# Expert feed-forward kernel: the sums of weights and of gathered rows move from GpSimd to VectorE

## The chip, the cores and the metric

The kernel runs on one core of one Trainium2 chip. The metric is the device time of one execution in microseconds (us), from three timed runs. One more execution was recorded by the hardware profiler; the rows quoted below are from that one.

## The reference, cut to what matters

The program computes a cross-attention layer and then a mixture of 8 experts, each a gated feed-forward network. Every one of the 4096 tokens goes to 2 experts. Only the second part is touched by the change:

```
x_rep_sort = take(x_flat, sort_idx // 2)              # rows gathered by expert
h   = silu(ragged_dot(x_rep_sort, w1)) * ragged_dot(x_rep_sort, w3)   # 1024 -> 3584
out = ragged_dot(h, w2)                                # 3584 -> 1024
out = sum over the token's 2 experts of weight * out
```

## The kernel before, in words

`attend_and_route` does the attention and writes tables of rows by expert (the first 555 us). `experts` then works through slots. A slot is one expert with up to 1088 of its rows. With these inputs 8 slots are filled.

**Products.** Every fp32 operand is split into a high part and a low rest of type fp32r, and each product is made of three matmuls: high by high, high by low, low by high. ScalarE copies the high part (`weight_hi`, `w2_hi`, `h_hi`, `rows_hi`, all at L1042), and VectorE subtracts it from the operand to get the low part (`weight_lo`, `w2_lo`, `h_lo`, `rows_lo`, all recorded at L1238). The tiles are `wh`/`wl` for weights and hidden values and `xh`/`xl` for rows.

**Units.** The first half of a slot (matmul L1462) is 28 units, 14 column pairs of w1 and of w3 in turn (a = 0, 1). A unit is a 2x2 block product done with 7 products in place of 8 (Winograd's form of Strassen's scheme). So it needs four sums of weight blocks (`sums`, four buffers) and, once for a slot, four sums of blocks of gathered rows. VectorE combines the seven products from PSUM (L1241, L1275) and multiplies by the gate (L1261). While TensorE works on one unit, ScalarE and VectorE split the weights of the next: entry e of `wh`/`wl` is refilled once product e is done.

**Down passes.** The second half (matmul L1495) is 4 passes (c = 0 to 3) of 28 steps. A step t needs a tile of w2 (256 KB) and of the stored hidden values (272 KB). Its buffers are one of two: SyncE loads tile t once `w2_lo` and `h_lo` of t-2 are done, ScalarE splits it once TensorE finished step t-2. A step of TensorE has 12 matmuls in the slots with at most 512 columns (slots 0, 1, 3, 5, "narrow" below) and 24 in the others (2, 4, 6, 7, "wide"). After a pass the result is turned back (`turn_back`, L1562), multiplied (`rows_out`, L1332) and added to the output by five indirect DMAs (`scatter`, L1722). Within the passes the rows of the next slot are prepared: gathered by GpSimd's indirect DMAs (`gather`, L1704), turned by TensorE (`turn_rows`, L1543), copied by ScalarE into the four `sums` buffers, split, summed and split again. `rows_hi` and `rows_lo` stand between the steps in an order written out by hand.

**Who forms the sums before.** GpSimd, in `weight_sums` (L1653 to L1661), `row_sums` (L1668 to L1674) and `tail_sums` (L1681 to L1687, the last rows of a slot). GpSimd's queue in a slot is, in order: the weight sums of 13 pairs; records and the first gather; then for each pass c the gather for c+1, `row_sums` of c, in pass 1 `tail_sums`, and, for c > 0, `scatter` of pass c-1; then the first weight sums of the next slot, `scatter` of pass 3, and four more weight sums. `row_sums` waits for `rows_lo` 0 and then 2 of the same pass, and `tail_sums` for `tail_lo` 0 and 2, so each `scatter` stands in the queue behind these. In pass 3 SyncE also loads the next expert's first weights (`load13`, L972, two DMAs of 1 MB each), one behind the loads of step 7 and one behind those of step 15.

Of the kernel before, what the change touches and what calls it, by code (L numbers as in the profile page):

```python
# [21 lines left out]
P = 128  # L22
# [803 lines left out]
def experts(nc, w1, w3, w2, out, x2_rows, table, meta, raw13, s_raw13):  # L826

    with ExitStack() as st:
# [405 lines left out]
        def _(dve):  # L1234
# [7 lines left out]

            def weight_lo(s, i, a, e):
# [8 lines left out]
            def unit(s, i, a, cols, after):  # L1252
# [96 lines left out]
            def down_phase(s, cols):  # L1349
# [7 lines left out]
                for c in range(4):  # L1357
# [3 lines left out]
                    rows_lo(n + c, c, 1, steady)  # L1361
                    steps(t + 4, t + 5)
                    rows_lo(n + c, c, 2, steady)
                    for i in range(3, EP):
                        steps(t + 2 * i, t + 2 * i + 2) if i > 3 else steps(t + 5, t + 8)
                        rows_lo(n + c, c, i, steady)
                    if c == 1:
                        steps(t + 14, t + 15)
                        for i in range(3):
                            tail_lo(s + 1, i)  # L1370
                        steps(t + 15, t + 16)
                        for i in range(3, EP):
                            tail_lo(s + 1, i)
                        steps(t + 16, t + MT)
                    else:
                        steps(t + 14, t + MT)
# [12 lines left out]
            def slot(s, cols):  # L1389

                with dve.Fori(0, PAIRS - 1) as i:
                    unit(s, i, 0, cols, lambda e: weight_lo(s, i, 1, e))
                    unit(s, i, 1, cols, lambda e: weight_lo(s, i + 1, 0, e))
                i = PAIRS - 1
                unit(s, i, 0, cols, lambda e: weight_lo(s, i, 1, e))
# [7 lines left out]
                unit(s, i, 1, cols, begin_down)  # L1403
# [22 lines left out]
            for c in range(4):  # L1426
                for i in range(EP):
                    rows_lo(c, c, i, first_q[c % 2])
            for i in range(EP):
# [202 lines left out]
        def _(pool):  # L1632
# [7 lines left out]
            def weight_sums(s, i, a, fresh=False):  # L1640

                A11, A12, A21, A22 = (raw13[a][:, kh * KH:(kh + 1) * KH, mt * P:(mt + 1) * P]
                                      for mt in range(2) for kh in range(2))
                before = s * PRODUCTS + i * (2 * EP) + a * EP - EP
                done = s * (PAIRS * 8) + i * 8 + a * 4
                pool.wait_ge(s_raw13[a], s * (PAIRS * 16) + i * 16 + 16)

                def free(e):
                    if not fresh:
                        pool.wait_ge(s_wlo, before + e + 1)  # L1650

                free(1)
                G.tensor_tensor(sums[:, 0, :, :], A11, A21, ALU.subtract).then_inc(s_sum, 1)  # L1653
                free(4)
                G.tensor_tensor(sums[:, 1, :, :], A21, A22, ALU.add).then_inc(s_sum, 1)  # L1655
                pool.wait_ge(s_sum, done + 2)
                free(2)
                G.tensor_tensor(sums[:, 2, :, :], sums[:, 1, :, :], A11, ALU.subtract).then_inc(s_sum, 1)  # L1658
                pool.wait_ge(s_sum, done + 3)
                free(5)  # L1660
                G.tensor_tensor(sums[:, 3, :, :], A12, sums[:, 2, :, :], ALU.subtract).then_inc(s_sum, 1)  # L1661

            def row_sums(n, quads):

                x11, x21, x12, x22 = quads
                pool.wait_ge(s_quad, n * 4 + 4)
                pool.wait_ge(s_xlo, n * EP + 1)
                G.tensor_tensor(x11, x12, x11, ALU.subtract).then_inc(s_xsum, 1)  # L1668
# [181 lines left out]
```

## Time and profile before

| | us |
|---|---|
| median of 3 runs | 8200.89 |
| lowest, highest | 8200.25, 8223.35 |
| profiled execution, device time | 8231.72 |
| its span, first to last instruction | 8230.1 |

| engine | busy us | share |
|---|---|---|
| TensorE matmul | 7729.7 | 94% |
| VectorE | 4379.1 | 53% |
| ScalarE | 3009.0 | 37% |
| GpSimd | 2138.8 | 26% |

The page's busy shares are means over parts of the kernel that differ. A row of the chain of waits names what TensorE's start was waiting for in the end. In a line of a group, the number after the bar is busy time, then the mean of one instruction in ns, then the idle time of the engine just before these instructions, with what ended it.

### The profile page before, as it was taken

The page shows a single profiled execution, that of the slowest core. Times are in us where ns is not written, and L with a number is a line of the kernel's source. Part 1 is how long each engine was busy: PE and PEld are TensorE (multiplying, and loading weights), DVE is VectorE, ACT ScalarE, POOL GpSimd, SP SyncE. Part 2 cuts the span into 40 slices and gives each one's busy share as a digit, 9 for nine tenths or more (in the row PEclk, how much of TensorE's full clock was granted, in tenths as well). Part 3 has the DMA queues.
Part 4 walks back from the last instruction along what each step waited for, and adds up shares of the span by engine and source line. Part 5 has one row for each costly group of instructions (what it writes and reads, how often), then busy time and mean ns, then how long its engine had stood idle before and what let it go on. Part 6 is the DMA issues. An engine that isn't in the chain of part 4 may idle for free.

```text
span 8230.1 us, 143438 instructions
## 1 busy us (share of the span) xinstructions
PE 7729.7 (94%) x47421; PEld 6882.5 (84%) x47422; DVE 4379.1 (53%) x6153; ACT 3009.0 (37%) x5051; POOL 2138.8 (26%) x1752
## 2 busy tenths in 40 slices
PE   8949999899999999999999999899999999999997
PEld 5538877788779999888779999888778999999997
DVE  6765555555555545555554545455554554545454
ACT  2323334333443334333443334333343333433343
POOL 2343322232222221223212221223222221122212
PEclk8969999999999999999999999999999999999999
DMA  3322246322652236422562225522463225622255
GB/s 113 120 79 78 83 130 193 107 89 85 193 157 78 78 114 183 120 89 79 161 191 79 76 77 182 161 81 82 135 193 99 78 78 165 185 76 75 78 184 153
DMA packets 606830, 979.04 MB, mean 119 GB/s; under 512 B 45152, under 2 KB 281072, under 8 KB 606576
## 3 DMA queue, kind: packets, MB, share of 16 engines
q1 hardware_dynamic: 571696, 902.21, 34.0%
q0 software_dynamic: 34880, 74.14, 4.0%
q8 instruction: 74, 1.21, 0.1%
q14 instruction: 180, 1.47, 0.1%
HBM read 783.93 MB, written 194.35 MB: 119 GB/s over the span
## 4 chain that ended last, share of the span: by engine, by line
PE 79%; DMA 5%; DVE 4%; issue 2%; ACT 1%; SPq 0%; POOL 0%; DVEq 0%; ACTq 0%; POOLq 0%
PE pair L1462 54%; PE pair L1495 24%; DVE wl L1238 3%; DMA raw<-hd 2%; DMA raw<-in_L_ffn_w 2%; ACT wh L1042 1%; DMA part<-hd 1%; PE pair L1543 1%; PE pair L1562 0%; DVE hid L1332 0%; SPq L978 0%; DVE xl L1238 0%; DMA w_last<-in_L_ffn_w 0%; DVE part L1332 0%; DMA part<-x_rows,id_g 0%
## 5 line engine op out<-in xcount | busy, mean ns | idle before, releaser
L1462 PE MATMUL pair<-xh,wh 128*128 128x264 f32 (+3 forms) x9408 | 2513.6, 321 | 96.7 <-issue 57.7
L1462 PE MATMUL pair<-xh,wl 128*128 128x264 f32 (+3 forms) x9408 | 2516.2, 322 | 0.0
L1462 PE MATMUL pair<-xl,wh 128*128 128x264 f32 (+3 forms) x9408 | 2512.1, 321 | 0.0
L1238 DVE TENSOR_TENSOR wl<-raw,wh 128x512 fp32r<-128x512 f32 x2019 | 1524.9, 775 | 1833.7 <-ACT wh L1042 1805.2
L1042 ACT ACTIVATE wh<-raw 128x512 fp32r<-128x512 f32 x2019 | 1233.5, 631 | 1909.2 <-PE pair L1495 772.3
L1462 PEld LDWEIGHTS pair<-xh,wh 128*128 128x128 f32 x9408 | 1578.6, 190 | 226.4 <-issue 83.3
L1462 PEld LDWEIGHTS pair<-xh,wl 128*128 128x128 f32 x9408 | 1574.2, 189 | 127.7
L1462 PEld LDWEIGHTS pair<-xl,wh 128*128 128x128 f32 x9408 | 1574.2, 189 | 124.4
L1495 PE MATMUL pair<-wh 128*128 128x264 f32 (+3 forms) x5376 | 1251.4, 328 | 225.8 <-DVE wl L1238 182.5
L1495 PE MATMUL pair<-wh,wl 128*128 128x264 f32 (+3 forms) x5376 | 1444.7, 323 | 0.0
L1495 PE MATMUL pair<-wl,wh 128*128 128x264 f32 (+3 forms) x5376 | 1444.3, 323 | 0.0
L1042 ACT ACTIVATE wh<-sums 128x512 fp32r<-128x512 f32 x900 | 567.3, 632 | 1626.8 <-PE pair L1462 1561.2
L1495 PEld LDWEIGHTS pair<-wh 128*128 128x128 f32 x5376 | 848.5, 190 | 367.9 <-issue 282.6
L1495 PEld LDWEIGHTS pair<-wh,wl 128*128 128x128 f32 x5376 | 906.6, 191 | 72.5
L1495 PEld LDWEIGHTS pair<-wl,wh 128*128 128x128 f32 x5376 | 907.9, 191 | 69.0 <-issue 0.2
L1238 DVE TENSOR_TENSOR wl<-sums,wh 128x512 fp32r<-128x512 f32 x900 | 686.5, 764 | 389.6 <-ACT wh L1042 371.9
L1653 POOL TENSOR_TENSOR sums<-raw 128x512 f32<-128x512 f32 x225 | 295.4, 1313 | 1776.0 <-DMA raw<-in_L_ffn_w 1060.2
L1655 POOL TENSOR_TENSOR sums<-raw 128x512 f32<-128x512 f32 x225 | 339.6, 1510 | 1222.9 <-DVE wl L1238 1222.9
L1241 DVE TENSOR_TENSOR part<-part,pair 128x512 f32<-128x512 f32 (+2 forms) x448 | 312.7, 698 | 556.0 <-PE pair L1462 554.7
L1638 POOL TENSOR_TENSOR ticks<-ticks 128x1 f32<-128x1 f32 x92 | 47.0, 511 | 1427.5 <-PE pair L1543 829.4
L1658 POOL TENSOR_TENSOR sums<-sums,raw 128x512 f32<-128x512 f32 x225 | 347.4, 1544 | 34.9 <-POOL sums L1655 34.2
L1238 DVE TENSOR_TENSOR wl<-w_last,wh 128x512 fp32r<-128x512 f32 x224 | 169.6, 757 | 341.2 <-ACT wh L1042 341.2
(245 smaller groups left out, 5305.5 us busy)
## 6 DMA issues: line engine op xcount, KB each, us to landing
raw<-in_L_ffn_w SPq DMA_DIRECT2D x226, 1024.0 KB, 6.6
raw<-hd SPq DMA_DIRECT2D x672, 272.0 KB, 3.3
raw<-in_L_ffn_w SPq DMA_DIRECT2D x672, 256.0 KB, 3.0
hd<-hid SPq DMA_DIRECT2D x112, 1088.0 KB, 5.2
part<-hd SPq DMA_DIRECT2D x224, 272.0 KB, 3.2
w_last<-in_L_ffn_w SPq DMA_DIRECT2D x224, 256.0 KB, 3.0
xin<-in_x SPq DMA_DIRECT2D x8, 2048.0 KB, 9.9
out_x<-x SPq DMA_DIRECT2D x32, 512.0 KB, 2.7
```

The costliest lines, as they stand in the source:

```text
L1042: return nc.scalar.activation(out, in_, ACT.Copy)
L1238: return V.tensor_tensor(out, a, b, ALU.subtract)
L1241: return V.tensor_tensor(out, a, b, ALU.add)
L1462: mm = pe.matmul(to[:, c, 0:hi - lo], entry(w, e)[:, ks], x[:, e, k, lo:hi], start=begin and k == 0 and i == 0, stop=k == KH - 1 and i == ...
L1495: mm = pe.matmul(pair[d][:, ch, 0:hi - lo], down_w(w, par)[:, d * P:(d + 1) * P], down_h(h, par)[:, lo:hi], start=begin, stop=end, skip_gr ...
L1543: mm = pe.transpose(pair[q][:, side, k * P:(k + 1) * P], xs[nh][:, at:at + P], ident[:, :])
L1638: G.tensor_tensor(ticks[:, 0:1], ticks[:, 0:1], ticks[:, 1:2], ALU.add).then_inc(s_tick, 1)
L1653: G.tensor_tensor(sums[:, 0, :, :], A11, A21, ALU.subtract).then_inc(s_sum, 1)
L1655: G.tensor_tensor(sums[:, 1, :, :], A21, A22, ALU.add).then_inc(s_sum, 1)
L1658: G.tensor_tensor(sums[:, 2, :, :], sums[:, 1, :, :], A11, ALU.subtract).then_inc(s_sum, 1)
```

## The change

All these sums are formed by VectorE. GpSimd keeps the gathers, the scatters and the small copies. In the units, the four weight sums of the next half pair stand between the combining operations (`following(0)` to `following(3)`). In the passes, row sum 0 stands behind `rows_lo` 1, and row sums 1 to 3 behind steps 5, 6 and 7 one by one; the tail sums stand behind `tail_lo` 2 in pass 1; the first four weight sums of the next slot stand behind steps 21, 23, 25 and 27 of pass 3. The order of the operands in each sum is unchanged. On GpSimd the waits that stood inside the sums fall away with them, and one wait is new, ahead of the records. SyncE, ScalarE and TensorE keep their instructions.

```diff
+            def weight_sum(s, i, a, n, fresh=False):
...
+                if not fresh:
+                    dve.wait_ge(s_wlo, s * PRODUCTS + i * (2 * EP) + a * EP - EP + (1, 4, 2, 5)[n] + 1)
+                if n == 0:
+                    dve.wait_ge(s_raw13[a], s * (PAIRS * 16) + i * 16 + 16)
+                    less(sums[:, 0, :, :], A11, A21).then_inc(s_sum, 1)
...
+            def row_sum(n, quads, i):
+                x11, x21, x12, x22 = quads
+                if i == 0:
+                    dve.wait_ge(s_quad, n * 4 + 4)
+                    dve.wait_ge(s_xlo, n * EP + 1)
+                    less(x11, x12, x11).then_inc(s_xsum, 1)
...
+                following(0)
                 after(0)
+                following(1)
                 after(1)
+                following(2)
                 product_done(s, i, a, 2)
                 dve.wait_ge(s_s1, g + 1)
                 plus(in_sbuf(u2, cols), in_sbuf(s1, cols), in_psum(b2, cols)).then_inc(s_u2, 1)
+                following(3)
                 after(2)
...
                     rows_lo(n + c, c, 1, steady)
+                    row_sum(n + c, steady, 0)
                     steps(t + 4, t + 5)
                     rows_lo(n + c, c, 2, steady)
-                    for i in range(3, EP):
-                        steps(t + 2 * i, t + 2 * i + 2) if i > 3 else steps(t + 5, t + 8)
+                    steps(t + 5, t + 6)
+                    for i in range(1, 4):
+                        row_sum(n + c, steady, i)
+                        steps(t + 5 + i, t + 6 + i) if i < 3 else None
+                    rows_lo(n + c, c, 3, steady)
+                    for i in range(4, EP):
+                        steps(t + 2 * i, t + 2 * i + 2)
                         rows_lo(n + c, c, i, steady)
...
                         for i in range(3):
                             tail_lo(s + 1, i)
+                        tail_sums(s + 1)
...
+                        steps(t + 14, t + 20)
+                        for k in range(4):
+                            steps(t + 20 + 2 * k, t + 22 + 2 * k)
+                            weight_sum(s + 1, 0, 0, k, fresh=True)
...
@@ GpSimd, slot
-                with pool.Fori(0, PAIRS - 1) as i:
-                    weight_sums(s, i + 1, 0)
-                    weight_sums(s, i + 1, 1)
-
+                pool.wait_ge(s_wlo, s * PRODUCTS + (PRODUCTS - 3 * EP))
                 tick(s * 11 + 4)
...
                         gather(c + 1, xg, s_xg)
-                    row_sums(s * 4 + 4 + c, steady)
-                    if c == 1:
-                        tail_sums(s + 1)
                     if c > 0:
                         scatter(s, c - 1, width, s * 11 + (10, 12, 13)[c - 1])
-                pool.wait_ge(s_xlo, s * (4 * EP) + 8 * EP)
-                weight_sums(s + 1, 0, 0, fresh=True)
                 scatter(s, 3, width, s * 11 + 14)
-                weight_sums(s + 1, 0, 1)
```

Ahead of slot 0 the same holds: VectorE forms the four row sums of each of the four groups of rows behind `rows_lo` 2 of that group, then `rows_lo` 3 to 6, and the tail sums likewise; GpSimd there has only gathers.

## Rows read from the trace of the kernel before

**Rows 1.** The page, busy time, share and instructions of each engine
```profile
PE 7729.7 (94%) x47421; PEld 6882.5 (84%) x47422; DVE 4379.1 (53%) x6153; ACT 3009.0 (37%) x5051; POOL 2138.8 (26%) x1752
```

**Rows 2.** Groups by line, TensorE: first matmul of each unit product, of each down step
```profile
L1462 PE MATMUL pair<-xh,wh 128*128 128x264 f32 (+3 forms) x9408 | 2513.6, 321 | 96.7 <-issue 57.7 <-DVE xl L1238 20.5 <-DVE wl L1238 13.9
L1495 PE MATMUL pair<-wh 128*128 128x264 f32 (+3 forms) x5376 | 1251.4, 328 | 225.8 <-DVE wl L1238 182.5 <-DVE part L1332 22.3 <-issue 10.4
```

**Rows 3.** Stretches, last line: narrow passes 1 and 2; wide; narrow 3; wide 3
```profile
sum 671.96, PE 633.99; mean PE 79.25
...
sum 699.41, PE 673.18; mean PE 84.15
...
sum 361.52, PE 321.31; mean PE 80.33
...
sum 385.45, PE 345.21; mean PE 86.30
```

**Rows 4.** The same, steps 20 to 26 of the 12 narrow, of the 12 wide
```profile
sum 232.68, PE 231.90; mean PE 19.33
...
sum 247.95, PE 247.95; mean PE 20.66
```

**Rows 5.** Timeline, VectorE, slot 0, pass 1: start, us, what [idle before]
```profile
1249.61 1.29 DVE L1238 TENSOR_TENSOR xl<-sums,xh 128x512 fp32r<-128x512 f32 x2
1251.23 3.06 DVE L1238 TENSOR_TENSOR wl<-raw,wh 128x512 fp32r<-128x512 f32 x2 [0.33 <-ACT wh L1042]
1258.42 1.29 DVE L1238 TENSOR_TENSOR wl<-raw,wh 128x512 fp32r<-128x512 f32 x2 [1.22 <-ACT wh L1042]
```

**Rows 6.** Timeline, GpSimd: a row sum there, and the first DMA of two scatters
```profile
1250.38 1.68 POOL L1668 TENSOR_TENSOR sums<-sums 128x512 f32<-128x512 f32 x1 [9.15 <-DVE xl L1238]
...
1284.71 1.71 POOL L1722 DMA_INDIRECT out_x<-hid,id_s  x1 [0.40 <-issue]
...
1432.36 1.90 POOL L1722 DMA_INDIRECT out_x<-hid,id_s  x1 [0.15 <-issue]
```

**Rows 7.** Timeline, TensorE, slot 0: a stall in pass 1, three of pass 3
```profile
1254.69 0.49 PE L1495 MATMUL pair<-wh 128*128 128x496 f32 x1 [1.55 <-DVE wl L1238]
...
1447.13 2.02 PE L1495 MATMUL pair<-wh 128*128 128x496 f32 x4 [7.54 <-DVE wl L1238]
1466.89 1.16 PE L1495 MATMUL pair<-wh 128*128 128x496 f32 x4 [1.29 <-DVE wl L1238]
...
1474.67 1.15 PE L1495 MATMUL pair<-wh 128*128 128x496 f32 x4 [1.71 <-DVE wl L1238]
```

**Rows 8.** Chain of waits, slot 0, pieces that are loads: start, us
```profile
1257.50 3.06 DMA raw<-in_L_ffn_w
...
1286.34 4.82 DMA raw<-hd
...
1434.23 11.05 DMA part<-hd
...
1467.30 5.53 DMA part<-hd
```

**Rows 9.** One line's instructions, L1238: ns min/median/max
```profile
L1238 DVE TENSOR_TENSOR wl<-raw,wh x2019: 668/693/1960, 557.7 to 8202.1; 128x512 fp32r<-128x512 f32 x155, 128x528 fp32r<-128x528 f32 x22, 128x544 fp32r<-128x544 f32 x7
```

**Rows 10.** Stretches: after the 7.54 us stall; within the units of slot 0
```profile
1447.10:1451.90 4.80, 4.77 (x13) 3.91 (x14) 1.99 (x3) 1.78 (x3) 0.00 (x0) 0.55 0.60 174
...
700.00:1100.00 400.00, 400.00 (x1797) 337.41 (x1796) 228.54 (x297) 146.62 (x236) 124.06 (x85) 1.00 0.27 88
```

**Rows 11.** Timeline, ScalarE, one group of rows ahead of slot 0
```profile
592.38 2.04 ACT L1042 ACTIVATE sums<-pair 128x512 f32<-128x512 f32 x4
...
597.41 0.63 ACT L1042 ACTIVATE xh<-sums 128x512 fp32r<-128x512 f32 x1 [1.44 <-POOL sums L1668]
...
602.42 0.63 ACT L1042 ACTIVATE xh<-sums 128x512 fp32r<-128x512 f32 x1 [1.04 <-POOL sums L1674]
```

**Rows 12.** Chain of waits, the first piece of the units
```profile
618.82 20.47 PE pair L1462 x84
```

More of the change, by code:

```diff
@@ L1241, in plus, with tail_sums @@
                 return V.tensor_tensor(out, a, b, ALU.add)
+            def weight_sum(s, i, a, n, fresh=False):
+                A11, A12, A21, A22 = (raw13[a][:, kh * KH:(kh + 1) * KH, mt * P:(mt + 1) * P]
+                                      for mt in range(2) for kh in range(2))
+                done = s * (PAIRS * 8) + i * 8 + a * 4
+                if not fresh:
[3 more added lines that the diff above has]
+                    less(sums[:, 0, :, :], A11, A21).then_inc(s_sum, 1)
+                elif n == 1:
+                    plus(sums[:, 1, :, :], A21, A22).then_inc(s_sum, 1)
+                elif n == 2:
+                    dve.wait_ge(s_sum, done + 2)
+                    less(sums[:, 2, :, :], sums[:, 1, :, :], A11).then_inc(s_sum, 1)
+                else:
+                    dve.wait_ge(s_sum, done + 3)
+                    less(sums[:, 3, :, :], A12, sums[:, 2, :, :]).then_inc(s_sum, 1)
+            def row_sum(n, quads, i):
[4 more added lines that the diff above has]
+                    less(x11, x12, x11).then_inc(s_xsum, 1)
+                elif i == 1:
+                    less(x12, x22, x12).then_inc(s_xsum, 1)
+                elif i == 2:
+                    dve.wait_ge(s_xsum, n * 4 + 1)
+                    dve.wait_ge(s_xlo, n * EP + 3)
+                    less(x22, x22, x11).then_inc(s_xsum, 1)
+                else:
+                    dve.wait_ge(s_xsum, n * 4 + 3)
+                    less(x21, x21, x22).then_inc(s_xsum, 1)
+            def tail_sums(s):
+                x11, x21, x12, x22 = (tail(q) for q in range(4))
+                dve.wait_ge(s_tq, s + 1)
+                dve.wait_ge(s_tlo, s * EP + 3)
+                less(x11, x12, x11).then_inc(s_tsum, 1)
+                less(x12, x22, x12).then_inc(s_tsum, 1)
+                dve.wait_ge(s_tsum, s * 4 + 1)
+                less(x22, x22, x11).then_inc(s_tsum, 1)
+                dve.wait_ge(s_tsum, s * 4 + 3)
+                less(x21, x21, x22).then_inc(s_tsum, 1)
             def weight_lo(s, i, a, e):
@@ L1250, in product_done, with unit @@
                 dve.wait_ge(s_prod, s * PRODUCTS + i * (2 * EP) + a * EP + e + 1 + EP)
-            def unit(s, i, a, cols, after):
+            def unit(s, i, a, cols, after, following):
                 g = s * UNITS2 + i * 2 + a
@@ L1401, in begin_down @@
                         h_lo(s, e - 3, cols)
-                unit(s, i, 1, cols, begin_down)
+                unit(s, i, 1, cols, begin_down, lambda n: None)
                 down_phase(s, cols)
@@ L1426, in _ @@
             for c in range(4):
-                for i in range(EP):
+                for i in range(3):
                     rows_lo(c, c, i, first_q[c % 2])
-            for i in range(EP):
+                for i in range(4):
+                    row_sum(c, first_q[c % 2], i)
+                for i in range(3, EP):
+                    rows_lo(c, c, i, first_q[c % 2])
+            for i in range(3):
+                tail_lo(0, i)
+            tail_sums(0)
+            for i in range(3, EP):
                 tail_lo(0, i)
@@ L1638, in tick @@
                 G.tensor_tensor(ticks[:, 0:1], ticks[:, 0:1], ticks[:, 1:2], ALU.add).then_inc(s_tick, 1)
[L1640 to L1661, printed above, removed]
@@ L1802, in _ @@
                 gather(c + 2, first_x[c], s_xfirst[c + 2])
-                row_sums(c, first_q[c])
             pool.wait_ge(s_xt, 12)
@@ L1806, in _ @@
             gather_tail(s_xfirst[4])
-            for c in (2, 3):
-                row_sums(c, first_q[c % 2])
-            tail_sums(0)
-            pool.wait_ge(s_xlo, 4 * EP)
-            weight_sums(0, 0, 1)
             with pool.Fori(0, SLOTS) as s:
```

31 lines of the change are left out of this document (5 added, 26 removed).

## The prediction, made before the changed kernel was run

> **What bounds the kernel now.** I read the page's busy shares first, then the groups by line, then stretches, and last the timelines around the stalls. TensorE is busy 94% of the span and VectorE 53% [rows 1]. The 9408 unit products start without waiting, but for 96.7 us in all, of which 57.7 us is its own issue; the down steps lose 225.8 us, 182.5 of them to VectorE's low parts [rows 2]. So the units are bound by TensorE, and what can be won or lost by another order of VectorE lies in the passes and ahead of slot 0.
>
> How much lies there: in calm stretches (7 steps in each of 12 passes) a narrow step takes 232.68/84 = 2.770 us and a wide one 247.95/84 = 2.952 us [rows 4]. Passes 1 and 2 (four slots each kind, 224 steps) last 671.96 and 699.41 us, against 620.5 and 661.2 at the calm pace: 51.5 and 38.2 us too long. Pass 3 (112 steps) lasts 361.52 and 385.45 us against 310.2 and 330.6: 51.3 and 54.9 us too long [rows 3]. The excess is 195.9 us over 24 passes.
>
> Where it comes from, read in slot 0:
> - At step 4 of a pass TensorE waits 1.55 us [rows 7]. Just before, VectorE does two row splits in 1.29 us, then two low parts in 3.06 us, where the same pair takes 1.29 us a little later [rows 5]. In that moment GpSimd forms a row sum, 1.68 us long [rows 6]. The median of such a low part is 693 ns, the longest 1960 [rows 9].
> - Where `scatter` runs, loads take longer: 4.82 us against 3.06 [rows 8]. The load loop of one buffer (load 3.06, ScalarE, VectorE's pair 1.3, issue) turns over in about 5.45 us, two narrow steps in 5.54 us, so a late load becomes a stall. `scatter` of pass 0 starts at 1284.71 [rows 6], about 42 us into pass 1 (whose step 0 lies four steps before 1254.69 - 1.55), since `row_sums` and `tail_sums` stand ahead of it; in passes 2 and 3 only `row_sums` does.
> - In pass 3 this order puts `scatter` at 1432.36 [rows 6], where SyncE issues a 1 MB load of weights. A step's load then takes 11.05 us [rows 8] and TensorE stalls 7.54 us [rows 7]. After it TensorE's granted clock is 0.55 of full, near its 1.2 GHz level, for 4.8 us [rows 10], which costs another 2 us. The second 1 MB load, with no scatter beside it, gives a load of 5.53 us [rows 8] and a stall of 1.71 us [rows 7]. The 1.29 us stall before that is once more GpSimd's sums (the first weight sums of the next slot) beside VectorE.
>
> **The change, part by part.**
>
> *Units.* 55 sets of four weight sums for a slot pass from GpSimd to VectorE: 220 x 0.61 us (the pitch of back-to-back low parts; two take 1.29 [rows 5]) = 134 us a slot. In 400 us of units VectorE is busy 228.54 us [rows 10]. A unit lasts 18.8 us, the addition is 2.4 us, so its share goes from 57% to about 70%, less what was stretching by GpSimd. The order matters more than the share: products 4 and 6 wait for u2 and c22, and each has one whole product, 2.7 us, in which VectorE may be late. The new sums stand ahead of u2 while product 2 still runs, or behind it. I take 0. If the cover were gone, one sum late in each of 224 units costs 0.61 us x 224 = 137 us; that end I keep for the range of the slower rival only. The loads of raw weights are a unit ahead, and stay so.
>
> *Stretching in the passes.* Here the sums are 16 row sums, 4 small tail sums and 4 weight sums a slot. Row sum 0 adds 0.61 us ahead of the pair that before took 3.06 us and would take 1.29: step 4's low parts are ready 1.1 us sooner (1251.5 + 1.3 = 1252.8 against 1254.3), and TensorE ends step 3 at about 1253.1. The stall of 1.55 us would be gone, if the load is there. In pass 0, where no scatter follows, I take 1.0 us x 8 = 8 us.
>
> *Scatter moved.* In GpSimd's queue `scatter` of c-1 now stands right behind the gather of c+1, in pass 3 behind nothing. It starts 2 to 3 us into the pass and slows loads in the first 16 us: steps 4 to 6. The start of a pass has 1 to 2 us of spare time in the loads, as TensorE has just turned rows. I expect a stall of about 2.5 us narrow and 1.7 wide there, no second one by the scatter later, and 0.5 us for the tail. With what is left of other waits I take an excess of 3.2 us for each of the 8 narrow passes 1 and 2 and 2.2 for the wide: 25.6 and 17.6 instead of 51.5 and 38.2. Won: 25.9 + 20.6 = 46.5 us. Bounds: nothing won here if the scatter costs as much as both stalls did, and 75 us if the spare time swallows it.
>
> *Pass 3.* Scatter ends before the first 1 MB load begins. The two 1 MB loads then cost about as much as the second one does now, 1.7 us each, and the sums no longer stretch: 1.7 + 1.7 + the scatter's 2.5 (narrow) or 1.7 (wide) + 0.5 = 6.5 and 5.5 us. Over 4 + 4 passes 26 and 22 instead of 51.3 and 54.9. Won: 25.3 + 32.9 = 58.2 us. Bounds: 30 us if each 1 MB load alone costs twice that, and 80 us.
>
> *VectorE's own price.* The passes get 24 operations a slot, 20 of full size: 160 x 0.61 = 98 us in all. They stand singly in gaps like the 1.22 us in which VectorE waits for ScalarE [rows 5]; only behind step 7 (a sum and a row split, 1.28 us) and at the tail (about 2.4 us) does it get tight. I take a fifth as exposed: 20 us. Bounds: 0 and 98 us.
>
> *Ahead of slot 0.* A group of rows takes 10.7 us (592.38 to 603.05): 2.04 us of copies and three splits on ScalarE, then four splits that wait for GpSimd's sums, 5.01 us from the start of the first to that of the last, 1.67 each [rows 11]. With VectorE the group is 11 operations x 0.61 = 6.7 us plus some latency, 7.2 us in all. Four groups give 4 x 3.5 = 14 us; the first has gathers to wait for, so I take 13. Bounds: 5 and 18. The gathers keep ahead, since no sums stand between them on GpSimd.
>
> *Ends.* GpSimd's last four weight sums stood behind the last scatter, whose DMAs land at about the same time. I take 0.
>
> **The Trainium skill.** The stretch at step 4 is an extra 1.07 us on one low part beside a 1.68 us sum, not a doubling of everything [rows 5, 6]. The page "SBUF — State Buffer", section "SBUF: two separate sides", says that VectorE with two SBUF inputs and a GpSimd operation that reads SBUF take the shared ports as a lock, and the later one waits for the whole instruction. By that rule a pair would lose nearly the whole sum, 1.7 us each time, by the row 1.07 to 1.8; the removal would be worth up to 0.6 us a stall more, in 32 passes 19 us. The same section warns that a DMA issued by GpSimd starves while VectorE runs in a mode that uses both ports, and names copies for it. Were that true for these subtractions too, a fuller VectorE would draw the scatters out; they take 1.71 to 1.90 us each beside VectorE's work [rows 6], so the trace shows little of it.
>
> **The sum.** 46.5 + 58.2 + 8 + 13 - 20 = 105.7 us won. On the profiled execution's own 8231.7 us this gives 8126 us. That one lies 30.8 us above the median of the runs, and I take the same difference from the median: 8200.9 - 105.7 = 8095 us.
>
> **The rivals.**
> - *A, the stalls only move* (0.13): gather, scatter and the refilling of the loads meet at the start of a pass, and passes 1 and 2 win nothing; pass 3 wins 30 us, pass 0 and the start 21, VectorE costs 10: 41 us won, 8160 us. For it: narrow steps have only 0.1 us in 5.5 to spare. Against it: behind the gather at the start of pass 1 a load takes 3.06 us again at 1257.50 [rows 8].
> - *B, VectorE becomes the bound of the load loop* (0.07, the slower side): each sum delays a low part, that delays SyncE's next load of that buffer, and TensorE waits. The price is 98 us in the passes plus half of the 137 us in the units (those behind which u2 is late), against 8 + 13 won and some 50 of the moved scatters: 98 + 68 - 71 = 95 us, 8296 us. It decides from the point where what is added in a step exceeds VectorE's gap, 1.22 us; the sums are 0.61. Only the tail passes that point.
> - *C, no change* (0.08): GpSimd's sums stretched VectorE where it hid, and the early scatter costs what pass 3 gains; only the 13 us at the start are left, 8188 us. Against it stands the 7.54 us stall, which needs scatter and a 1 MB load together.
> - *D, more is won* (0.12): the early scatter hides wholly and the clock never falls in pass 3. 75 + 80 + 8 + 18 = 181 less 10: 8030 us.
>
> **How the numbers follow.** The forecast has 0.60; its own range is 8060 to 8140, from the bounds of its terms taken together. A and D fill the sides. The range of 8 in 10 is 8035 to 8165. A measurement of this kernel can tell 0.3%, 25 us, from no change. Faster by more than that: forecast, A and D, 0.85. Within: C, 0.08. Slower: B, 0.07.
>
> **What would show it.** In the changed profile: low parts of weights with a longest near 0.7 us in the passes; no stall at step 4 of pass 0; `scatter` within 3 us of each pass's start; in pass 3 no load of 11 us, and no stretch at half clock after a stall of 7 us; an excess of 24 passes near 91 us plus VectorE's 20; TensorE's first unit matmul at about 606 us in place of 618.82 [rows 12]; units as long as before. The forecast is wrong if unit products wait for VectorE, if steps 5 to 8 or the tail's steps stall by more than 1 us, or if loads at the start of a pass take over 7 us.

## The result, and the profile after

The changed kernel takes 8158.19 us (median of 5 runs, 8149.4 to 8164.92); the kernel before, timed beside it, 8205.15 (5 runs). The ratio is 0.9937, 95% interval [0.9922, 0.9952]; the medians differ by 47 us. The forecast was 106 us faster. So the direction and the range were right, and the size was 2.2 times too large. The profiled execution lasted 8157.62 us, 74.1 less than the profiled one of before.

Page after, busy time of each engine: GpSimd's 2138.8 us are 593.5, VectorE has gained 215 us [rows 1].

```profile
PE 7720.2 (95%) x47421; PEld 6898.2 (85%) x47422; DVE 4594.0 (56%) x7229; ACT 2989.2 (37%) x5051; POOL 593.5 (7%) x672
```

Groups by line after, TensorE. The unit products still don't wait for VectorE (31.8 us, before 34.4 [rows 2]); the down steps (now L1566) have lost 72 us of idle time that VectorE's low parts ended.

```profile
L1533 PE MATMUL pair<-xh,wh 128*128 128x264 f32 (+3 forms) x9408 | 2513.6, 321 | 102.6 <-issue 62.5 <-DVE xl L1238 16.4 <-DVE wl L1238 15.4
L1566 PE MATMUL pair<-wh 128*128 128x264 f32 (+3 forms) x5376 | 1242.5, 326 | 157.5 <-DVE wl L1238 110.3 <-DVE part L1384 22.4 <-issue 15.3
```

Stretches after, last lines, in the order of [rows 3]: narrow passes 1 and 2; wide; narrow 3; wide 3. Three of the four are 24 to 26 us shorter. The second, wide passes 1 and 2, is 1.8 us shorter, where 20.6 were forecast.

```profile
sum 647.76, PE 625.93; mean PE 78.24
...
sum 697.63, PE 678.19; mean PE 84.77
...
sum 337.74, PE 315.50; mean PE 78.88
...
sum 359.85, PE 340.63; mean PE 85.16
```

The low parts of weights after, ns min/median/max. The longest was 1960 [rows 9].

```profile
L1238 DVE TENSOR_TENSOR wl<-raw,wh x2019: 668/692/777, 563.2 to 8129.4; 128x512 fp32r<-128x512 f32 x155, 128x528 fp32r<-128x528 f32 x22, 128x544 fp32r<-128x544 f32 x7
```

Timeline after, slot 0, pass 1, which begins at 1233.68: GpSimd's first scatter DMA, then VectorE at steps 3 to 5, then TensorE's waits. The row splits and the sum run at full speed and the pair takes 1.37 us [rows 5]; the scatter stands 1.3 us behind the start of the pass and not 42 [rows 6]. TensorE no longer waits at step 4 for a stretched pair, but at steps 3 and 4 for low parts of late loads.

```profile
1235.00 1.75 POOL L1744 DMA_INDIRECT out_x<-hid,id_s  x1 [0.34 <-issue]
```
```profile
1243.68 1.28 DVE L1238 TENSOR_TENSOR xl<-sums,xh 128x512 fp32r<-128x512 f32 x2
1244.89 0.68 DVE L1238 TENSOR_TENSOR sums<-sums 128x512 f32<-128x512 f32 x1
...
1248.96 1.37 DVE L1238 TENSOR_TENSOR wl<-raw,wh 128x512 fp32r<-128x512 f32 x2 [0.77 <-ACT wh L1042]
```
```profile
1233.68 1.16 PE L1566 MATMUL pair<-wh 128*128 128x496 f32 x4 [1.12 <-DVE hid L1384]
1243.91 0.46 PE L1566 MATMUL pair<-wh 128*128 128x496 f32 x1 [1.85 <-DVE wl L1238]
1248.00 1.16 PE L1566 MATMUL pair<-wh 128*128 128x496 f32 x4 [1.15 <-DVE wl L1238]
```

A wide pass shows where the missing 19 us are. Slot 7, pass 1, TensorE's waits, first before, then after. Before there are 1.18 us at step 4, where the chain of waits names a low part stretched to 1.80 us by one of GpSimd's sums, and 1.33 us and 0.76 us where the scatter stood. After there is one wait, as long as the first two, and the pass is no shorter (86.71 us, before 86.33).

```profile
7925.98 1.25 PE L1495 MATMUL pair<-wh 128*128 128x264 f32 x8 [1.18 <-DVE wl L1238]
7968.62 1.23 PE L1495 MATMUL pair<-wh 128*128 128x264 f32 x8 [1.33 <-DVE wl L1238]
...
7972.53 0.49 PE L1495 MATMUL pair<-wh 128*128 128x264 f32 x2 [0.76 <-DVE wl L1238]
```
```profile
7863.44 1.52 PE L1566 MATMUL pair<-wh 128*128 128x264 f32 x8 [2.56 <-DVE wl L1238]
```

The stretched low part in the chain of waits before:

```profile
7923.79 1.80 DVE wl L1238
```

The cause of the 2.56 us in the chain of waits after (start, us): a load of 6.57 us beside the scatter, its high part, its low part. Behind the stall comes the clock. The row of stretches (length, busy time of TensorE, its weight loads, VectorE, ScalarE, GpSimd, then the granted clock) shows 0.60 of full for 4.3 us, so most of it at the 1.2 GHz level, which costs some 1.7 us (0.40 of 4.26). In the 11 us from the tenth of a pass on, the granted clock is below 1.00 in 7 of 24 passes after, in 1 of before and in none of no_add (below).

```profile
7855.00 6.57 DMA raw<-hd
...
7861.65 0.65 ACT wh L1042
...
7862.32 0.72 DVE wl L1238
...
7863.44 16.56 PE pair L1566 x121
```
```profile
7863.44:7867.70 4.26, 4.26 (x22) 4.26 (x23) 2.19 (x4) 1.28 (x2) 0.00 (x0) 0.60 0.50 159
```

Pass 3 of slot 0 after, TensorE's waits. The 7.54 us stall is gone [rows 7]. In its place are 3.37 us beside the scatter and 1.92 and 1.49 beside the two 1 MB loads.

```profile
1418.22 1.16 PE L1566 MATMUL pair<-wh 128*128 128x496 f32 x4 [3.37 <-DVE wl L1238]
1431.22 1.17 PE L1566 MATMUL pair<-wh 128*128 128x496 f32 x4 [1.92 <-DVE wl L1238]
...
1455.20 1.16 PE L1566 MATMUL pair<-wh 128*128 128x496 f32 x4 [1.49 <-DVE wl L1238]
```

Ahead of slot 0, chain of waits after: two groups of rows begin 7.6 us apart, before 10.7 [rows 11], and the first unit starts at 612.71 [rows 12].

```profile
592.74 2.04 ACT sums L1042 x4
...
600.33 2.04 ACT hid L1042 x4
...
612.71 21.30 PE pair L1533 x84
```

**The account**, from the two profiled executions. Forecasts are those of the parts. VectorE's own price (+20) can't be seen apart; it lies in the four rows of passes.

| part | forecast | first pair | second pair |
|---|---|---|---|
| start of experts to first unit | -13 | -11.5 | -12.9 |
| pass 0, narrow and wide | -8 | -9.7 | -11.6 |
| passes 1 and 2, narrow | -25.9 | -24.2 | -17.4 |
| passes 1 and 2, wide | -20.6 | -1.8 | -11.4 |
| pass 3, narrow | -25.3 | -23.8 | -1.5 |
| pass 3, wide | -32.9 | -25.6 | -24.3 |
| VectorE's price in the passes | +20 | within | within |
| the 8 slots' units | 0 | +14.1 | +11.5 |
| all else | 0 | +8.3 | -4.2 |
| sum | -105.7 | -74.1 | -71.7 |

The second pair are the two kernels profiled again (b_again and a_again, below), in a lot in which the kernel before was 38 us slower than beside the result. "All else" is what lies ahead of the experts and between the parts. The rows are rounded one by one.

Pass 0 keeps 61.5 us above the calm pace after the change, and 57.4 even in no_add (below). In all 8 slots TensorE waits 2.1 to 7.1 us there at step 2, which the change did not touch; its cause was not looked into.

### The profile page after: what moved, and what is told of

Read it like the earlier page. It is cut to its first block, busy times and chain, and to the rows that moved or that the text cites. A ratio compares the mean times of both kernels' runs of the same rounds, so it can differ in the third digit from the quotient of the medians.

```text
span 8156.0 us, 143302 instructions
## 1 busy us (share of the span) xinstructions
PE 7720.2 (95%) x47421; PEld 6898.2 (85%) x47422; DVE 4594.0 (56%) x7229; ACT 2989.2 (37%) x5051; POOL 593.5 (7%) x672
## 4 chain that ended last, share of the span: by engine, by line
PE 83%; DMA 4%; DVE 2%; issue 2%; ACT 1%; SPq 0%; POOL 0%; DVEq 0%; ACTq 0%; POOLq 0%
PE pair L1533 55%; PE pair L1566 28%; DMA raw<-hd 2%; DMA part<-hd 1%; DVE wl L1238 1%; ACT wh L1042 1%; PE pair L1614 1%; DVE hid L1384 0%; PE pair L1633 0%; SPq L978 0%; DMA raw<-in_L_ffn_w 0%; DVE xl L1238 0%; DVE part L1384 0%; DMA part<-x_rows,id_g 0%; POOL out_x L1744 0%
## 5 line engine op out<-in xcount | busy, mean ns | idle before, releaser
L1238 DVE TENSOR_TENSOR wl<-raw,wh 128x512 fp32r<-128x512 f32 x2019 | 1349.4, 693 | 1662.7 <-ACT wh L1042 1661.4
L1042 ACT ACTIVATE wh<-raw 128x512 fp32r<-128x512 f32 x2019 | 1215.2, 629 | 1895.9 <-PE pair L1566 1008.2
L1566 PE MATMUL pair<-wl,wh 128*128 128x264 f32 (+3 forms) x5376 | 1448.6, 324 | 0.0
L1566 PE MATMUL pair<-wh,wl 128*128 128x264 f32 (+3 forms) x5376 | 1448.2, 324 | 0.0
L1566 PE MATMUL pair<-wh 128*128 128x264 f32 (+3 forms) x5376 | 1242.5, 326 | 157.5 <-DVE wl L1238 110.3
L1566 PEld LDWEIGHTS pair<-wh 128*128 128x128 f32 x5376 | 847.0, 190 | 272.7 <-issue 187.4
L1566 PEld LDWEIGHTS pair<-wl,wh 128*128 128x128 f32 x5376 | 912.7, 192 | 71.7 <-issue 0.2
L1566 PEld LDWEIGHTS pair<-wh,wl 128*128 128x128 f32 x5376 | 910.7, 192 | 72.0
L1238 DVE TENSOR_TENSOR wl<-sums,wh 128x512 fp32r<-128x512 f32 x900 | 617.5, 688 | 256.7 <-ACT wh L1042 243.8
L1241 DVE TENSOR_TENSOR sil<-part,pair 128x512 f32<-128x512 f32 (+2 forms) x336 | 234.4, 698 | 254.2 <-PE pair L1533 250.4
L1238 DVE TENSOR_TENSOR wl<-w_last,wh 128x512 fp32r<-128x512 f32 x224 | 154.9, 692 | 314.0 <-ACT wh L1042 313.7
L1241 DVE TENSOR_TENSOR hid<-part,pair 128x512 f32<-128x512 f32 (+2 forms) x336 | 234.4, 698 | 117.3 <-PE pair L1533 111.7
L1042 ACT ACTIVATE wh<-w_last 128x512 fp32r<-128x512 f32 x224 | 141.6, 632 | 395.8 <-PE pair L1566 318.6
```

The lines of the kernel that those rows point to most:

```text
L1042: return nc.scalar.activation(out, in_, ACT.Copy)
L1238: return V.tensor_tensor(out, a, b, ALU.subtract)
L1241: return V.tensor_tensor(out, a, b, ALU.add)
L1566: mm = pe.matmul(pair[d][:, ch, 0:hi - lo], down_w(w, par)[:, d * P:(d + 1) * P], down_h(h, par)[:, lo:hi], start=begin, stop=end, skip_gr ...
```

## The experiments

They ran in three lots of four kernels, the first two on one chip, the last (split and those below it) on another. In all three the kernel before lay at 8241.5 to 8243.3 us, and each ratio is to the runs of before in its own lot. The forecast's method counts how far passes 1 to 3 are above the calm pace (2.770 and 2.952 us a step, front of the prediction); the columns give this excess, in us, from one profiled execution each.

| kernel | median us | ratio to before, 95% | 1, 2 narrow | 1, 2 wide | 3 narrow | 3 wide | sum | units |
|---|---|---|---|---|---|---|---|---|
| before again | 8249.53 | 1.0003 [0.9994, 1.0012] | 55.2 | 47.1 | 52.4 | 59.6 | 214.3 | 4520.4 |
| changed again | 8184.03 | 0.9930 [0.9917, 0.9944] | 37.8 | 35.7 | 50.9 | 35.3 | 159.7 | 4531.9 |
| late_scatter | 8184.08 | 0.9924 [0.9911, 0.9938] | 40.8 | 33.8 | 49.4 | 46.1 | 170.1 | 4540.0 |
| early_scatter | 8215.08 | 0.9964 [0.9951, 0.9978] | 50.6 | 38.7 | 42.9 | 40.8 | 173.0 | 4523.1 |
| no_add | 8094.48 | 0.9819 [0.9805, 0.9833] | 6.8 | 8.3 | 22.0 | 30.8 | 67.9 | 4522.0 |
| small_sums | 8179.17 | 0.9921 [0.9907, 0.9935] | 36.4 | 38.7 | 43.2 | 34.0 | 152.3 | 4530.7 |
| passes_only | 8181.10 | 0.9928 [0.9914, 0.9942] | 40.5 | 34.6 | 44.4 | 39.4 | 158.9 | 4524.4 |
| spaced | 8170.45 | 0.9911 [0.9896, 0.9927] | 40.9 | 26.2 | 40.0 | 35.0 | 142.1 | 4526.0 |
| split | 8131.40 | 0.9872 [0.9856, 0.9889] | 25.8 | 22.8 | 37.0 | 31.2 | 116.8 | 4536.0 |
| split_before | 8184.55 | 0.9937 [0.9923, 0.9951] | 36.4 | 37.9 | 36.6 | 37.2 | 148.1 | 4517.8 |
| split_spaced | 8093.35 | 0.9821 [0.9802, 0.9840] | 15.7 | 12.3 | 26.5 | 16.4 | 70.9 | 4531.4 |
| three | 8083.12 | 0.9816 [0.9800, 0.9831] | 11.2 | 9.9 | 25.4 | 12.9 | 59.4 | 4525.3 |

**Both kernels again.** No edit.

> The kernel before, unchanged, profiled a second time. Theory 1 (the first profile is no usual execution): the 24 passes 1 to 3 are less than 195.9 us above the calm pace, by 20 us or more, most of it in steps 6 to 12 of pass 3, where the scatter meets the 1 MB load; the time is about 8205 us and the units differ by less than 6 us. Rival (the spread lies elsewhere): the excess stays within 8 us of 195.9, and the difference is in the units or ahead of them.

> The changed kernel, unchanged, profiled a second time. Time 8158 us, within 10. If the profile is a usual one, the passes 1 to 3 are again 120 us above the calm pace, within 8, and the wide passes 1 and 2 again hold 36 of it. Rival: the wide passes' 36 us was chance, and they come out near the 18 us that were forecast.

Both kernels ran 26 to 44 us longer than beside the result, so both forecasts of the time were missed, and those of the excess too: it was 214.3 us, neither 20 us below 195.9 nor within 8 of it, and 159.7, not 120. Only the changed kernel's wide passes 1 and 2 came as expected, 35.7. The ratio came out the same (0.9930 beside 0.9937). Units and start repeat to 3 us. The parts of the passes don't: pass 3 narrow gained 23.8 us in the first pair and 1.5 in the second, while wide passes 1 and 2 gained more. A single stretch of one profiled execution is good to some 20 us here, the sum of all passes to about 19 (-85.0 and -66.1).

**Where the scatter stands.** late_scatter is the changed kernel with the scatter held back to about where it stood before; early_scatter is the kernel before with the scatter ahead of the row sums.

```diff
                     if c > 0:
+                        pool.wait_ge(s_xsum, (s * 4 + 4 + c) * 4 + 3)
+                        if c == 1:
+                            pool.wait_ge(s_tsum, s * 4 + 8)
                         scatter(s, c - 1, width, s * 11 + (10, 12, 13)[c - 1])
```
```diff
+                    if c > 0:
+                        scatter(s, c - 1, width, s * 11 + (10, 12, 13)[c - 1])
                     row_sums(s * 4 + 4 + c, steady)
                     if c == 1:
                         tail_sums(s + 1)
-                    if c > 0:
-                        scatter(s, c - 1, width, s * 11 + (10, 12, 13)[c - 1])
```

> The changed kernel, but GpSimd's scatter in passes 1 to 3 waits until the third row sum of the pass is done (in pass 1, the last tail sum), so about where it stood before; the sums stay on VectorE. Theory O (the order of GpSimd's queue carries the gain): 30 to 50 us of it go, 8190 to 8210 us, the 1 MB load and the scatter meet again and a load takes about 10 us. Theory S (the end of the stretching carries it): 8150 to 8165 us, as changed.

> The kernel before, but with the scatter of pass c-1 ahead of the row sums of pass c in GpSimd's queue; all sums stay on GpSimd. Theory O: it wins 25 to 45 us on the kernel before, 8160 to 8180 us. Theory S: no change, 8195 to 8215 us. Rival to both: the sums, now 10 us later behind five DMAs, hold ScalarE up at its fourth row split, and it is slower than before.

With GpSimd's sums, the early scatter is worth 28 us (8215.08 against 8243.3). With VectorE's sums it is worth nothing (8184.03 against 8184.08). VectorE's sums are worth 59 us with a late scatter and 31 with an early one. Each of the two theories so holds in one run and fails in the other: the two gains overlap, and the forecast had added them. Pass 3 of the wide slots has the same order: its excess is 59.6 with neither, 46.1 and 40.8 with one, 35.3 with both; differences this small lie within the 20 us of a single stretch, so the medians carry the point.

The corner late_scatter isn't quite the old place. Before, the first scatter DMA of pass 3 goes out within 0.2 us of the first 1 MB load. In late_scatter SyncE reaches that load sooner and the scatter follows 2.4 to 3.8 us behind it. SyncE's 1 MB load and GpSimd's first scatter DMA in slot 0, pass 3, before and in late_scatter:

```profile
1432.49 0.38 SPq L972 DMA_DIRECT2D raw<-in_L_ffn_w  x1
```
```profile
1416.61 0.38 SPq L972 DMA_DIRECT2D raw<-in_L_ffn_w  x1
```
```profile
1419.29 2.02 POOL L1744 DMA_INDIRECT out_x<-hid,id_s  x1 [0.53 <-issue]
```

The step's load then takes 6.59 us and not 11.05 [rows 8], and the stall at step 8 is 1.0 to 4.4 us in the eight slots, in the two profiles of before 3.8 to 8.8. So part of what VectorE's sums are worth with a late scatter can be that the two transfers no longer start together; a scatter held exactly at the 1 MB load with VectorE's sums was not run. early_scatter and the changed kernel have the scatter at the same places, so the 31 us between them are free of this.

**The scatter's whole price.** no_add sends the rows to indices out of bounds, so that nothing is added to the output: the addition of the experts' results is left out.

```diff
-                add(0, row(0))
-                add(1, row(1))
+                add(0, nowhere[:, 0:1])
+                add(1, nowhere[:, 0:1])
```

> The changed kernel with all scatters aimed at a row out of bounds: GpSimd issues the five DMAs, they carry nothing, so the addition of the experts' output is left out. Theory L (what is left of the stalls is the scatters' traffic wherever it stands, because the load loop has no slack): the passes 1 to 3 lose 90 us or more of their excess of about 130 to 160 us, and the time is 80 to 120 us below the changed kernel, ratio to before near 0.98. Rival (what is left is the refilling after the turn, the 1 MB loads and VectorE's own order): less than 40 us below the changed kernel.

GpSimd issues the same DMAs in the same time (median 1.58 us, in the changed kernel 1.57). Without their traffic the kernel takes 90 us less than the changed one, as Theory L had it, and passes 1 and 2 fall almost to the calm pace: 37.8 to 6.8 us narrow, 35.7 to 8.3 wide, 3.9 and 3.4 us a pass. The forecast had put the scatter at 2.5 and 1.7. In slot 7, pass 1, the chain of waits has one piece where the changed kernel has the 6.57 us load:

```profile
7771.43 16.60 PE pair L1566 x122
```

What is left in pass 3 is the 1 MB loads: from the start of step 6 to that of step 18 the four narrow passes are 20.9 us too long and the wide 28.3, 2.6 and 3.5 us for each load. The forecast had 1.7. The changed kernel beside the result has 14.3 and 13.2 us there, 1.8 and 1.7 for each, and profiled again 32.7 and 19.6, 4.1 and 2.5, so the same load costs different times in different executions.

**VectorE's own price.** small_sums forms the row sums over 128 of 512 columns only, so the rest of the rows' sums is left out. passes_only gives the weight sums inside the units back to GpSimd.

```diff
-                x11, x21, x12, x22 = quads
+                x11, x21, x12, x22 = (q[:, 0:1, :] for q in quads)
```
```diff
-                pool.wait_ge(s_wlo, s * PRODUCTS + (PRODUCTS - 3 * EP))
+                with pool.Fori(0, PAIRS - 1) as i:
+                    weight_sums(s, i + 1, 0)
+                    weight_sums(s, i + 1, 1)
```

> The changed kernel with each row sum in the passes formed over 128 of its 512 elements (the rest of each row sum is left out): same instructions and waits, each some 0.4 us shorter, 51 us of VectorE in all. Theory 3 (VectorE's own price): 10 to 40 us below the changed kernel. Rival (they stand in VectorE's gaps, price 0): within 8 us of the changed kernel, ratio to before 0.992 to 0.994.

> The changed kernel with the weight sums of the units back on GpSimd; row sums, tail sums and the first weight sums of a slot stay on VectorE. Theory U (the sums in VectorE's unit loop cost at the loop's first turn, where their code is fetched): the first units of slots 3 to 7 are as short as before, 5 to 12 us won on the changed kernel, the other units to the hundredth as long. Rival (the units are bound by TensorE throughout, the 12 us are chance): the same as the changed kernel within 5 us.

136 row sums of 0.29 us instead of 0.68, 54 us less work, take 5 us off the median, inside its uncertainty, and 5.0 us off the passes (2785.5 to 2780.5). By this the 98 us of VectorE's added work cost 0 to some 9 us (an estimate from 5 for 54), and not the 20 that were forecast. In passes_only the units are 7.5 us shorter, and no time that can be told is won (3 us).

Where the units' part comes from: in the changed kernel VectorE enters the first unit of slot 3 late. Timeline, first operation there, in the changed kernel and in "three" (sums of units on GpSimd, below):

```profile
3385.70 0.69 DVE L1238 TENSOR_TENSOR sums<-raw 128x512 f32<-128x512 f32 x1 [18.01 <-issue]
```
```profile
3358.30 0.69 DVE L1239 TENSOR_TENSOR wl<-raw,wh 128x512 fp32r<-128x512 f32 x1 [15.63 <-ACT wh L1043]
```

The slot's units began at 3367.9 and 3342.8, so VectorE is 17.8 us behind in the one and 15.5 in the other, and the first unit takes 33.2 us against 28.5. With sums inside the units it took 32.9 to 34.6 us in seven executions (30.6 in no_add), without them 27.4 to 29.2 in six. In the changed kernel the idle time is booked to issue, with nothing awaited; in "three" it is booked to a high part of ScalarE, whose own first work there comes behind 13.24 us booked to issue. That it is the fetching of a longer loop was not shown.

**The scatter spread out.** spaced holds each of the five DMAs of a scatter back to a step of its own.

```diff
                 def add(j, rows):
                     p = TAIL if j == 4 else P
+                    if at is not None:
+                        pool.wait_ge(s_hlo, s * STEPS + (c + 1) * MT + at[j] + 3)
+                        G.tensor_tensor(spare[:, c * 5 + j:c * 5 + j + 1], ticks[:, 1:2], ticks[:, 1:2], ALU.add)
...
-                        scatter(s, c - 1, width, s * 11 + (10, 12, 13)[c - 1])
+                        scatter(s, c - 1, width, s * 11 + (10, 12, 13)[c - 1],
+                                (10, 12, 19, 21, 23) if c == 3 else (6, 9, 12, 18, 21))
```

> The changed kernel with the five DMAs of each scatter of passes 0 to 2 issued one by one, each when TensorE's operands of a given step are ready: steps 6, 9, 12, 18, 21 of passes 1 and 2, steps 10, 12, 19, 21, 23 of pass 3, clear of the 1 MB loads. Theory L says that one DMA at a time delays a load by 1 us or so and wide slots absorb it: wide passes 1 and 2 near 18 us of excess in place of 36, narrow ones as now or a little better, 20 to 40 us below the changed kernel. Rival (each delay is lost, as the sum of traffic is the same): within 8 us of the changed kernel.

Wide passes 1 and 2 win 9.5 us, narrow ones lose 3, pass 3 wins 11, each within what one execution can tell, and the interval of the ratio (0.9896 to 0.9927) overlaps that of the changed kernel (0.9917 to 0.9944). So the win, 14 us in the medians, is less than the 20 to 40 of Theory L, and not clear of nothing. It fits a load loop with little slack: wide steps have spare time (two last 5.90 us, the load loop 5.45), narrow ones have almost none (5.54), and slowing five loads a little would only help where each has spare time of its own.

**The load loop without slack.** That pointed at the loop itself. In split SyncE issues the load of a w2 tile behind w2's own low part and no longer behind the hidden values' too; split_before is the same edit in the kernel before, split_spaced has spaced's as well, and three has all this with the units' sums on GpSimd.

```diff
                 sp.wait_ge(s_w2lo, s * STEPS + c * MT + i2 * 2 + par + 1)
-                sp.wait_ge(s_hlo, s * STEPS + c * MT + i2 * 2 + par + 1)
                 load_w2(e, c, i2 * 2 + par, par)
+                sp.wait_ge(s_hlo, s * STEPS + c * MT + i2 * 2 + par + 1)
```

> The changed kernel with one edit: in the down passes SyncE issues the load of a w2 tile as soon as the low part of the w2 tile two steps before is done, and waits for the low part of the hidden values only after that. Before, it waits for both and then issues both loads. So the turn-over of one w2 buffer, about 5.45 us (load 3.05, high part, pair of low parts, issue), becomes shorter by one low part, 0.6 us; that of the hidden values' buffer stays. Theory L (the loop of load, high part, low part has no slack, so whatever delays a load becomes a stall, and the excess grows by it): half of the loads get 0.6 us of slack, the stalls after the scatters shrink by up to a third; excess of 24 passes 160 us in the changed kernel on that chip to about 130, 20 to 40 us in all, ratio to before 0.988 to 0.991. Rival (the loads are limited by what the DMA engines move, and the later of the two loads sets the step anyway): within 8 us of the changed kernel, ratio about 0.992 to 0.993.

> The kernel before with the same edit of SyncE alone (the w2 load goes out behind the low part of w2, the load of hidden values behind its own). Theory L (loop without slack): its stalls have more to do with a late pair, because GpSimd's sums stretch it by 1 to 1.8 us and its scatters stand late; an earlier w2 load takes part of both away. Excess of 24 passes from 214 to 170 to 190 us, ratio 0.994 to 0.997. Rival (the hidden values' load, the later one, sets the step): no change, 0.999 to 1.001, excess 205 to 220.

> The changed kernel with the five indirect DMAs of each scatter let go one by one in a pass (behind steps 6, 9, 12, 18, 21; in pass 3 behind 10, 12, 19, 21, 23), which alone had a ratio of 0.9911, and with the earlier w2 load. Theory L: both gains in part, excess of 24 passes 142 to about 115, ratio 0.987 to 0.989. Rival (loads limited by the DMA engines): as the spaced scatters alone, 0.990 to 0.992.

> The spaced scatters and the earlier w2 load, and the weight sums inside the units back on GpSimd, as before the change (the sums of the passes stay on VectorE). By the run with the units' sums on GpSimd alone the first unit of slot 3 gets its 5 us of fetched code back and units are 7 us shorter in all; time was the same within 3 us. Expected: within 8 us of the one with VectorE's sums in the units, rather below it; ratio 0.986 to 0.989 by theory L, 0.989 to 0.992 by the rival.

The edit earns 0.58 points of ratio on the changed kernel (0.9930 to 0.9872, about 48 us) and 0.63 on the kernel before (1.0000 to 0.9937, 52 us). The rival (loads limited by the DMA engines) is out, and the theory's own 20 to 40 us were too few. The changed kernel did not run in this last lot; its ratio was 0.9930 and 0.9937 in two others, outside 0.9872's interval. One moved line is so worth as much as the whole change. With the slack, spreading the scatter is worth 0.51 points (0.9872 to 0.9821, intervals that don't meet), where without it it was 0.19, with intervals that overlap. That fits the picture of a delayed load that is passed on whole. The sizes were missed, all to the same side: split_before has an excess of 148.1 us where 170 to 190 were expected, split_spaced 70.9 where 115 were and a ratio of 0.9821 for 0.987 to 0.989, "three" 0.9816 for 0.986 to 0.989. Why 0.6 us of slack on half of the loads wins so much was not worked out, and what else the earlier issue changes was not tested apart. Last lines of the stretches, "three", in the order of [rows 3]:

```profile
sum 631.67, PE 622.95; mean PE 77.87
...
sum 671.14, PE 671.13; mean PE 83.89
...
sum 335.61, PE 318.19; mean PE 79.55
...
sum 343.50, PE 335.21; mean PE 83.80
```

In wide passes 1 and 2 TensorE is now busy for all but 0.01 us of 671.14, and 26.5 us less than after the change. "three" is the fastest kernel of the study, 0.9816 [0.9800, 0.9831] of before; with all its additions it stands level with no_add, which leaves them out.

## Why the prediction was right or wrong

The kernel got faster, as forecast, but by less than half of it. By size, the steps that failed are these: the difference between profile and median was carried over from before (27 us); the scatter at the start of a wide pass was priced too low (26 us over the 12 wide passes 1 to 3 in the first pair, most of it hidden by the 20 us for VectorE that did not come); the units were taken at 0 (14 us). Behind the second stands the gain of two edits that was added up and overlaps.

**Right: what GpSimd's sums did to VectorE.** The longest low part is 777 ns, the stall at step 4 of pass 0 is gone (pass 0 gained 9.7 us, forecast 8), the start of the experts gained 11.5 (forecast 13), and early_scatter against changed (31 us) shows the sums' worth by itself. The Trainium skill, "SBUF — State Buffer", section "SBUF: two separate sides", has the one of the two engines that starts first hold the shared ports for its whole instruction while the other is blocked. The trace agrees. GpSimd's second sum before, slot 0, pass 1:

```profile
1252.01 1.73 POOL L1669 TENSOR_TENSOR sums<-sums 128x512 f32<-128x512 f32 x1
```

It ends at 1253.74, and the pair of low parts begun at 1251.23 ends at 1254.29 [rows 5], 0.55 us behind it. In the trace of before 469 of the instructions recorded at L1238 began while such a sum was running, with more than 0.2 us of it left; 468 of them ended 0.55 to 0.59 us behind the sum. So a low part loses what is left of the sum: the pair lost 1.77 us (3.06 for 1.29), 0.69 on the first and 1.07 on the second, and the prediction's 1.07 and its 1.7 by the rule are one and the same effect.

**Right: but for a slot's first, no unit waits for VectorE.** TensorE's waits for it in the units fell from 34.4 to 31.8 us. In a stretch of 400 us VectorE is busy 249 us, 62%, where about 70% was forecast, less the stretching. The stretching was the larger part: 864 more instructions in the units of 8 slots, 527 us at 0.61, added 241 us (2344.7 to 2585.9). They are 27 sets of four for a slot, 66 us, and not the prediction's 55 sets and 134 us; its 57% and 70% were worked out from a unit and don't hang on that count. Rival B, VectorE as the bound of the load loop, did not come: taking 54 us of its work away gave back 5.

**Wrong: the scatter at the start of a pass.** Forecast: "a stall of about 2.5 us narrow and 1.7 wide there, no second one by the scatter later". There is no second one, but the first costs 3.9 and 3.4 us a pass (changed again against no_add; the profile beside the result against no_add gives 2.6 and 3.5), the fallen clock in it. The failed step is "1 to 2 us of spare time in the loads": in the wide pass above a load was issued at 7855.00, in the midst of the scatter's five DMAs, and took 6.57 us, 3.5 more than usual, of which TensorE paid 2.56. The change removed 1.18 us of stretching and 1.33 and 0.76 us beside the scatter there, and put one stall of 2.56 and a clock of 0.60 in their place: rival A's picture, in the wide slots alone. The narrow ones had more to lose (51.5 us) and won as forecast.

**Wrong: two gains added that overlap.** The terms for the stretching and for the scatter were each read from rows in which both effects were present. The four corners (0, 28, 59 and 59 us) show it: once the sums are off GpSimd, moving the scatter from where late_scatter has it to the start of the pass earns nothing that can be measured. In pass 3 the 7.54 us stall was priced as the collision of scatter and 1 MB load, to be ended by moving the scatter. In late_scatter the five DMAs still fall on that load, 2.7 us behind its issue in slot 0, and the stall is 3.20 us.

**Not settled: the 1 MB loads,** 1.7 us forecast. Beside the result they cost that, 1.8 and 1.7; in later executions 2.5 to 4.1. **Too large: VectorE's price,** 20 us forecast, 0 to some 9 by small_sums. By luck it cancels most of what the wide passes 1 to 3 fell short (18.8 and 7.3 us), which is why the sum of all passes (-85.0) came near its forecast (-92.7) in the first pair. In the second (-66.1) it did not.

**Missing: the units,** +14.1 and +11.5 us. In the first pair 5.1 us stand in slot 3, whose first unit is late. Another 5.6 are slot 6, whose 28 units took 20.72 us each instead of 20.53 with the same instructions. Other executions show both paces in slots 4, 6 and 7, with and without the change (before again: 20.53 in 4 and 7, 20.72 in 6), so that part looks like chance.

**Wrong: the step from the profile to the median.** "I take the same difference from the median": the profiled execution of before lay 30.8 us above its median (26.6 above that of the five later runs), that of the changed kernel 0.6 below its own. So the profiles differ by 74 us and the medians by 47. In the lots that followed a profiled execution lay between 24 below its median (no_add) and 16 above (late_scatter), so nothing justified carrying 30.8 over. Of the 59 us missed, 27 are this step, 14 the units, 8 the passes and 10 the rest of the account.

**How the profile had shown it.** The load loop of 5.45 us was in the prediction, beside 5.54 us for two narrow steps, and was used against a rival only. SyncE's two waits, for both low parts, stand ahead of both loads in the kernel's lines. Asked what a late load costs when the loop has 0.1 us to spare, these two would have pointed to what split and split_before measured: the scatter is paid at either place, and less once the loop has slack.

## What to carry to other kernels

When a transfer delays a double-buffered load loop that turns over in the time of the work it feeds, moving the transfer moves the stall; give the loop slack first (issue each load behind its own release), and spreading the transfer pays after that, as here. Don't add gains read from stalls that have two causes: price one with the other in place, and keep the smaller. Compare a forecast with the median only through several executions, since one profiled execution can lie 30 us off.

## What the runs showed of the hardware that was not expected

- The scatter's cost is in what its DMAs move, not in GpSimd's time. no_add keeps the indirect DMAs and their issue and is 90 us faster. What the addition costs beyond moving the rows was not run.
- A VectorE instruction that starts beside a GpSimd sum loses the rest of that sum: 468 of 469 ended 0.55 to 0.59 us behind it. GpSimd's sums had cost VectorE some 290 us in the units alone (estimate, 527 less 241).
- TensorE's clock falls behind small stalls too, but not behind each: 2.56 us of waiting in slot 7, pass 1, were followed by 4.3 us at 0.60 of full, 3.37 us in slot 0, pass 3, by a granted clock of 1.00.
- Units of 528 columns (slots 4, 6 and 7) run at one of two paces, 20.53 or 20.72 us, for a whole slot, at a granted clock of 1.00 in both.
- VectorE's first instructions in the unit loop come up to 18 us behind the start of a slot's units, in the changed kernel with no wait shown; in slot 3 this costs TensorE 9 us before the change and 14 after (28.0 and 33.2 us for a unit of 19.5).
